# Gate rows of a mixture of experts spread by products of turned gates, and a new order of the first two images

## The reference

```
h = concat(cls_tok, fourier_features(x) @ W.T)            # (8, 1025, 64)
h = h + causal_attention(layernorm(h), WQ, WK, WV)
e = layernorm(h)
w = softmax(mean(e, axis=0) @ Wr + br)                    # gates: token x 8 experts, shared by all images
y = for each expert: relu(bn(relu(bn(e @ W1 + b1)) @ W2 + b2)) @ Wo + bo
h = h + sum over experts of w * y
```

## Time and profile before

| | us |
|---|---|
| three runs | 418.02, 421.12, 422.26 (median 421.12) |
| profiled execution, its own time | 418.62 |
| its span, first to last instruction | 416.8 |
| mean granted TensorE clock | 0.969 of full |
| PE busy | 371.0 (89%) |
| DVE, ACT, POOL busy | 274.4, 200.9, 116.8 |

### The profile page before, as it was taken

The page is one execution under the profiler, slowest core; times in us unless marked ns, Lnnn a source line. Parts: engine busy times, 40 slices in busy tenths (PEclk is TensorE's granted clock), DMA queues, the critical chain, the costliest instruction groups (busy, mean ns, idle before and its releaser), DMA issues. The chain is left out here.

```text
span 416.8 us, 8088 instructions
## 1 busy us (share of the span) xinstructions
PE 371.0 (89%) x2716; PEld 175.0 (42%) x2716; DVE 274.4 (66%) x582; ACT 200.9 (48%) x387; POOL 116.8 (28%) x197
## 2 busy tenths in 40 slices
PE   5887899999999999999999967857978999999985
PEld 3554244445345444434435434424456433333332
DVE  3132667777877977967967978797334365655665
ACT  0233255455555546546546555456714565556521
POOL 4050202415414414324325324226300730000000
PEclk9989699999999999999999999999958999999999
DMA  6989901801800900900000000000000010011112
GB/s 150 221 156 221 171 2 40 165 0 39 165 2 17 186 0 1 200 0 0 0 0 2 2 1 0 2 1 2 2 0 0 3 27 16 12 26 27 27 27 50
DMA packets 29085, 20.42 MB, mean 49 GB/s; under 512 B 12376, under 2 KB 28928, under 8 KB 29056
## 3 DMA queue, kind: packets, MB, share of 16 engines
q1 hardware_dynamic: 28448, 19.91, 23.7%
q10 hardware_dynamic: 608, 0.12, 0.2%
HBM read 17.93 MB, written 2.10 MB: 48 GB/s over the span
## 5 line engine op out<-in xcount | busy, mean ns | idle before, releaser
L777 DVE TENSOR_REDUCE rmax<-Sp 128x1 f32<-128x1024 f32 x64 | 78.2, 1222 | 27.4 <-PE Sp L1135 26.7
L1135 PE MATMUL Sp<-eT,G 64*64 64x512 f32 x512 | 70.6, 620 | 22.3 <-issue 18.1
L503 ACT ACTIVATE PT<-PTp 128x512 f32<-128x512 f32 (+2 forms) x96 | 43.5, 489 | 48.4 <-PE PTp L1150 48.2
L402 POOL TENSOR_SCALAR_AFFINE_SELECT EP<-EP 128x128 f32<-128x128 f32 x64 | 23.0, 360 | 149.1 <-ACT EP L556 149.1
L556 ACT ACTIVATE EP<-Sp,negm 128x128 f32<-128x128 f32 (+3 forms) x64 | 47.7, 745 | 24.0 <-DVE negm L779 23.5
L787 DVE SCALAR_TENSOR_TENSOR EP<-Sp,EP 128x128 f32<-128x128 f32 (+3 forms) x64 | 48.1, 751 | 15.4 <-PE PTp L1150 9.4
L1150 PEld LDWEIGHTS PTp<-ident,EP 128*128 128x128 f32 x288 | 31.8, 143 | 43.9 <-issue 36.9
L1150 PE MATMUL PTp<-ident,EP 128*128 128x128 f32 x288 | 45.3, 285 | 3.5 <-DVE EP L787 2.8
L1135 PEld LDWEIGHTS Sp<-eT,G 64*64 64x64 f32 x512 | 14.9, 132 | 49.6 <-issue 49.6
L1168 PE MATMUL MM<-PT,e 128*64 128x512 f32 (+1 forms) x192 | 34.2, 491 | 0.5 <-ACT PT L503 0.3
L979 DVE SCALAR_TENSOR_TENSOR PT<-PTp,negc,XW 128x512 f32<-128x512 f32 x30 | 21.1, 746 | 18.1 <-PE PTp L1305 12.3
(11 more groups left out here) (264 smaller groups left out, 585.8 us busy)
## 6 DMA issues: line engine op xcount, KB each, us to landing
XW<-in_x_dram SPq DMA_DIRECT2D x6, 1024.0 KB, 10.0
X<-in_x_dram SPq DMA_DIRECT2D x6, 1024.0 KB, 10.8
out_dram<-xc SPq DMA_DIRECT2D x16, 128.0 KB, 2.0
XW<-in_x_dram SPq DMA_DIRECT2D x2, 576.0 KB, 8.8
X<-in_x_dram SPq DMA_DIRECT2D x2, 576.0 KB, 14.2
XW<-in_x_dram SPq DMA_DIRECT2D x2, 448.0 KB, 11.7
X<-in_x_dram SPq DMA_DIRECT2D x2, 448.0 KB, 13.7
EP<-in_L_tok_W_dram SPq DMA_DIRECT2D x2, 144.0 KB, 3.2
```

Of the source, the lines that this page charges most:

```text
L402: pool.affine_select(out=blk_, in_=blk_, compare_op=ALU.is_ge, fill=0.0, base=0, pattern=[[-1, 128]], channel_multiplier=1).then_inc(tri_d ...
L503: return act.activation(dst, src, ACT.Copy)
L777: dve.reduce_max(rmax[:, t:t + 1], Sp[t % 2][:, :], AX).then_inc(max_done, 1)
L1135: ins = pe.matmul(Sp[t % 2][64 * s:64 * s + 64, CH * c:CH * c + CH], G[q][rows, 128 * t + 64 * s:128 * t + 64 * s + 64], eT[q][rows, :], **ON)
```

## The change

1. **Start.** The five products of the class token move from in front of image 2 to behind `g_pair(0, 0)`, into a bank of Sp, and the batch-norm rows go to Sp too. Both parts of image 2 now run with only the batch-norm rows between them, ahead of `e_turn`. `score(0, 0, 0)` now comes before `sr_turn`, which waits for `agT`. On ACT the copies of the class token's vectors move behind `g_copy`; on DVE the two steps for `w00` move behind the first image's attention.
2. **Gate rows.** POOL makes a constant `pick` at the start (two copies of 64x512). DVE writes the gates twice over into `gwp` (two products of 128x64 elements), PE turns them with four transposes (and one for the class token), ACT and DVE copy one half each to `wT`, and the gate rows of a pair are two products of 64 x 128 x 512, `pick` against `wT`, into Sp. ACT's copy to WB stays.
3. **Bias.** The bias product is made for two halves (16 products instead of 8) and moves from before the second layer norm to behind `layer2(0, 0)`, beside the softmax. The product with the gates is four of 128 columns and one of 64 instead of nine of 64, from the same `wT`; the nine transposes are gone.
4. **Order of the experts.** `layer1(1, 2)` moves in front of the last logits, `layer2(0, 1)` uses the banks M0 and M1, DVE's layer norm of the eighth image comes before the first logits' step, `c_l2` no longer waits for that step, and `layer1(1, 3)` moves behind `c_l3`. SP loads `bo` twice. POOL clears two more buffers.

```diff
-        wT = EPs[0:NEXP, 0:9 * 128]
-        gx = [EPs[:, 1152:2176]..., prod[...]]
+        wT = EPs[:, 0:CH]
+        wTc = EPs[0:NEXP, CH:CH + 128]
...
# POOL
+            pool.wait_ge(turn_high, 1)
+            for r in range(2):
+                rows = slice(64 * r, 64 * r + 64)
+                pool.tensor_copy(pick[rows, :, :, :], eye2[rows, 0:2 * NEXP].rearrange("p (c a s) -> p a c s", c=2, s=2)[:, :, :, r]
+                                 .unsqueeze(3).to_broadcast([64, NPAIR, 2, D])).then_inc(pool_steps, 1)
...
# DVE
             ln2_ss(b)
+            ln2_e(b)
             dve.wait_ge(pe_steps, nth("q_lf", 1))
...
-            ln2_e(b)
...
+            for r in range(2):
+                dve.tensor_tensor(gwp[:, :, r, 0:2 * NEXP]..., gl9[:, 0:NT, :]..., gs9[:, 2, 0:NT]..., ALU.mult)
+            dve.tensor_tensor(gw9[:, NT:NT + 1, :], ...)
+            dve.wait_ge(pe_steps, nth("q_wT", 1))
+            dve.tensor_copy(wT[:, 256:CH], M1[:, 0:256]).then_inc(dve_steps, 1)
+            dve.wait_ge(pe_steps, nth("q_bo", 1))
+            dve.tensor_tensor(bo2[0:2 * NEXP, :, :], ..., ALU.add).then_inc(dve_steps, 1)
-            def spread(i): ...
...
# PE, start
-            pe.wait_ge(act_steps, nth("c_e0Tc", 1))
-            pe.matmul(M1[:, 0:D], e0T[:, :], AT32[:, :], **ON)
...
+            for n in range(8):
+                y_part(1, n, 8)
+            pe.wait_ge(act_steps, nth("c_e0Tc", 1))
+            e_turn(0, 0)
+            g_pair(0, 0)
+            pe.wait_ge(act_steps, nth("bn_c2", 2))
+            for c in range(2):
+                pe.matmul(Q0[64 * c:64 * c + 64, 384:385], AT32[:, :], e0T[:, 0:1], **ON)
...
+            score(0, 0, 0)
+            pe.wait_ge(act_steps, nth("c_ag", 2))
             sr_turn(0, 0)
# PE, experts
             def weight_rows(i):
...
-                for t in range(NT):
-                    ins = pe.transpose((MM, Sp[0], Sp[1], MM)[i][:, 128 * t:128 * t + 128], gx[i % 2][:, t, :], ident[:, :])
+                for r in range(2):
+                    rows = slice(64 * r, 64 * r + 64)
+                    ins = pe.matmul(L1p[1 - i % 2][r], pick[rows, i, :, :], wT[rows, :], **ON)
...
             layer2(0, 0)
+            pe.wait_ge(h1_done, 14)
+            for c in range(2):
+                for e in range(NEXP):
+                    k = 24 * e + 8 - 8 * c
+                    ins = pe.matmul(L1p[0][0][0:2 * NEXP, D * c:D * c + D], c2sel[:, k:k + 16], Wof[0:64, e, :],
+                                    start=(e == 0), stop=(e == NEXP - 1))
+            ins.then_inc(pe_steps, 1)
+            pe.wait_ge(dve_steps, nth("q_w", 2))
+            for i in range(QG):
+                pe.transpose((M0, M1)[i // 2][:, 128 * (i % 2):128 * (i % 2) + 128], gwp[:, i, :, :], ident[:, :])
...
             weight_rows(0)
+            for i in range(QG):
+                pe.matmul(M0[:, 128 * i:128 * i + 128], wT[0:64, 128 * i:128 * i + 128], bo2[:, :, :], **ON)
+            pe.matmul(M1[:, 0:D], wTc[:, :], bo2[0:NEXP, 0, :], **ON).then_inc(pe_steps, 1)
             weight_rows(1)
+            layer2(0, 1)
             weight_rows(2)
+            layer2(0, 2)
             weight_rows(3)
```

More of the change, by code:

```diff
@@ L85, in tower @@
         e32 = [sb(f"e32_{i}", [128, NT, D]) for i in range(2)]
-        prod = sb("prod", [128, NT, 2, D])
+        gwp = sb("gwp", [128, QG, 2, 64])
+        pick = sb("pick", [128, NPAIR, 2, D])
+        bo2 = sb("bo2", [64, 2, D])
         xc2 = sb("xc2", [128, NT, D])
@@ L925, in _ @@
             body(0, 0, first=True)
+            dve.wait_ge(act_steps, nth("c_vecc", 2))
+            dve.wait_ge(dve_steps, nth("c_e0", 1))
+            dve.tensor_tensor(c1B[:, :], e0B[:, :], ag[:, 1, :], ALU.mult).then_inc(dve_steps, 1)
+            dve.wait_ge(dve_steps, nth("c_w00p", 1))
+            dve.reduce_sum(w00[:, :], c1B[:, :], AX).then_inc(dve_steps, 1)
             with dve.Fori(0, NB // 2 - 1) as j:
@@ L937, in _ @@
             ln2_centre(b)
-            dve.wait_ge(pe_steps, nth("k_eT", 1))
-            dve.tensor_tensor(bo_s[:, :], M0[0:NEXP, 288:288 + D], bo_s[:, :], ALU.add).then_inc(dve_steps, 1)
             ln2_ss(b)
+            ln2_e(b)
             dve.wait_ge(pe_steps, nth("q_lf", 1))
@@ L1283, in layer1 @@
                     pe.wait_ge(p_done, at(8 * NB - 1 + p))
-                if b == 1 and p == 2:
-                    pe.wait_ge(act_steps, nth("q_wTc", 2))
+                if (b, p) in ((1, 3), (2, 0)):
+                    pe.wait_ge(act_steps, nth("q_bcc", 6 - p if b == 1 else 4))
                 pe.wait_ge(h1_done, at(8 * b + 2 * p - 2))
@@ L1296, in layer2 @@
                 if b == 0 and p == 0:
-                    pe.wait_ge(pt_done, at(NCH * NB))
-                pe.wait_ge(t_done, at(8 * b + 2 * p - (2 if NPAIR * b + p >= NPAIR * (NB - 1) - 1 else 0)))
+                    pe.wait_ge(dve_steps, nth("c_m", 2))
+                elif b == 0 and p == 1:
+                    pe.wait_ge(dve_steps, nth("q_wbc", 1))
+                elif b == 0 and p == 2:
+                    pe.wait_ge(t_done, 2)
+                else:
+                    pe.wait_ge(t_done, at(8 * b + 2 * p - (2 if NPAIR * b + p >= NPAIR * (NB - 1) - 1 else 0)))
                 if (b, p) == (NB - 2, 3):
@@ L1374, in _ @@
                     rows = slice(64 * s, 64 * s + 64)
-                    ins = pe.matmul((M0, M1)[s][0:64, 384 + 8 * p:392 + 8 * p], W2f[rows, p, :], h1c[rows, p, :], **ON)
+                    ins = pe.matmul(PTp[s][0:64, 8 * p:8 * p + 8], W2f[rows, p, :], h1c[rows, p, :], **ON)
             ins.then_inc(pe_steps, 1)
-            pe.wait_ge(dve_steps, nth("c_m", 2))
+            pe.wait_ge(ot_done, at(2 * NB))
             e2_turn(b)
+            layer1(1, 2)
             pe.wait_ge(e2t_done, at(NB))
+            pe.wait_ge(dve_steps, nth("q_lga", 1))
             for i in range(QG):
@@ L1409, in _ @@
             ins.then_inc(pe_steps, 1)
-            layer1(2, 1)
+            layer1(1, 3)
+            layer2(0, 3)
+            layer1(2, 0)
             pe.wait_ge(act_steps, nth("c_y", 1))
             pe.transpose(M1[0:8, 192:192 + D], yTc[:, :], ident[0:64, 0:64]).then_inc(pe_steps, 1)
+            layer1(2, 1)
             layer3(0, 0)
```

180 lines of the change are left out of this document (73 added, 107 removed).

## The result

The changed kernel is slower: 425.29 us (median of 20 runs, 421.16 to 427.61) against 421.94 (20 runs, 418.02 to 425.92), ratio 1.0077 with a 95% interval of 1.0044 to 1.0109. That is a loss of 0.8%, clear of the noise but less than the one per cent that the prediction calls slower. The prediction was 415.4, faster; the range ended at 420.0.

The account below looks back on a forecast made before the run. PE bounds the tail, partly at 1.2 GHz; the first row maximum opens attention. Start 0.8 plus tail 3.8 make 4.6 off: 414.0 from the profiled 418.62, set at 415.4 from 420.0; range 411.0 to 420.0.

Parts of the forecast that it names:

- The start, 1.3 earlier at the first row maximum: Opening of attention: first row maximum at 37.5 against 38.78, with image 2 begun earlier and at full clock.
- The 0.8 that was to be left at the end: Start's net gain: 1.0 taken after the 43 to 49 slow stretch, less 0.2 for DVE's `w00` steps.
- Rival B: Start pays nothing, through slow clock in image 2's first part or a later slow stretch: 416.2 us, chance 0.20.
- unless a slow stretch takes it back: Attention: moving the first row maximum moves all of it, except where 1.2 GHz stretches such as 43 to 49 intervene.
- the rise of the clock between 312.7 and 315.6: Tail: PE unbroken from 309.5, so clock rises up to 2.9 us sooner than 315.6, third layer 4.5 to 3.0 earlier.
- the rule was weighed: Tail: whether removing 32 full transposes removes what raised the clock; late and absent rises were kept among the cases.
- C: Rival: tail's clock rises near 319 because bias products are narrow; tail gains 1.4, start 0.4: 418.2 us, chance 0.16.
- D: Rival: 1.2 GHz up to the third layer, 427 us, chance 0.08; decides from a rise after 322.4, 0.5 per us.
- The bias products, "1.7 at full, 3.4 at half clock": Tail, behind the first `layer2`: sixteen bias products on PE's path, 1.7 us at full clock or 3.4 at half.
- The sum from the first gate-row pair to the third layer, 11.05: Tail at full clock: 10.8 us of PE's own work plus 0.25 for a DVE add, ACT's copies and `gated` hidden.
- 3.8 for the tail: Third layer's first product 3.8 us earlier, between 4.5 and 3.0, as transposes and copy rounds go, less bias products.
- The base, 420.0: Time the gain was taken from: the average of four times, above the profiled 418.62 and below the median 421.12.

Follow-up runs that it names:

- the start alone: The kernel before with only the new order of the start, old tail kept: 421.76 against 422.34 us, ratio 1.0004.
- bo_early: The changed kernel with the sixteen bias products put back in front of the class token's turn: median 421.39 against 422.34 us for the kernel before.
- wait_fill: The changed kernel plus five groups of four unread 64x64x512 products in the tail: 416.54 against 422.34 us for the kernel before, ratio 0.9895.
- before_fill: The kernel before plus five groups of four unread 64x64x512 products in its tail: 423.49 against 421.51 us, ratio 1.0013.
- turn_fill: The changed kernel plus five groups of eight unread 128x128 transposes in the tail: 416.11 against 422.78 us for the kernel before, ratio 0.9869.
- fill_fit: The changed kernel, bias products early, unread products in tail, attention's start and idle steps of images 7 and 8: 410.58 against 422.49 us (before), ratio 0.9748.
- fill_more: The changed kernel, bias products early, unread products in tail, attention's start and nearly every step of images 7 and 8: 415.26 against 422.78 us (before).
- bo_wide: The changed kernel with an unread 64x64x64 companion product for the bias products, in another quadrant: 432.67 against 422.78 us for the kernel before, ratio 1.0237.
- narrow_fill: The changed kernel plus five groups in the tail, each one unread product 8 columns wide, 512 moving: 426.01 against 421.51 us for the kernel before.

## Why the prediction was wrong

- **The start, 1.3 earlier at the first row maximum:** right, 1.44 from the H copy on, with the predicted steps: image 2's two parts at full clock, PE without a wait for the load of X or for POOL's diagonal. For the load the prediction had a weak reason: the last two loads of X took 13.4 and 13.9 us in the kernel before, nearer the long end of 10.5 to 15.0 than the short one. The 0.8 that was to be left at the end is not seen: the start alone has ratio 1.0004, with an interval of 2 us either way that cannot tell 0.8 from nothing. Rival B (the time is given back to the clock) fits, but it was not shown.
- **The attention, which moves by what moves its beginning "unless a slow stretch takes it back":** the exception was the rule. Its slow stretches (6.8 or 20.5 us at 1.2 GHz) came and went among kernels with the same list of instructions there, and move it by 4 to 5 us. The prediction looked at one execution of the kernel before, among the best of its kind (0.969), and reckoned with no slow stretch in attention but the one at 43 to 49.
- **The tail, the rise of the clock between 312.7 and 315.6, because "PE is now unbroken from 309.5":** this is the step that failed. PE was unbroken from 305 to 322, and the clock rose at 332. The first second-layer product stands 6.0 us later in this execution than in the one of before (315.44 against 309.45), so on the prediction's scale the rise came at 326, and behind the last logits the clock was down for 18.5 us in place of 8.2. I took unbroken work as enough. What stood before the rise in the earlier trace rows were transposes and nothing else, and I had written that down where the rule was weighed and given a later rise 24 chances in 100, 16 for a rise near 319 (C) and 8 for none before the third layer (D). It is their mechanism, with D's place right and its decision point (a rise later than 322.4 costs) passed; the clock was back at 326 on that scale and not only at the third layer. By D's price of 0.5 per us of delay that is 1.8 later than before; with the 1.1 by which the sum below was too small it makes 2.9, and the third layer did come 2.9 later behind the last logits (25.72 against 22.82).
- **The bias products, "1.7 at full, 3.4 at half clock":** right in size, 3.59. What the prediction did not weigh is that they could have stayed off PE's path: put back in front of the layer norm they gave 3.9 us (`bo_early`), part of it by the clock.
- **The sum from the first gate-row pair to the third layer, 11.05:** at full clock it is 12.2 (`wait_fill`, 315.36 to 327.56), 1.1 more. PE shows no idle time in it. From the start of one group to the start of the next it is 1.01 to 1.06 where a gate-row pair is followed by a second layer and back, priced at 0.87, and the bias rows took 1.34, priced at 1.0: these terms were too small. Why a group takes longer there was not looked into.
- **A structural gain:** there is one. In `wait_fill` against `before_fill` it is some 1.5 to 2.5 us behind the last logits, by estimate. In the runs as they are, at equal time at 1.2 GHz the changed kernel would be some 1 us faster (mean 424.5 less 0.39 x 42.1 against 421.5 less 0.39 x 32.1); the 10 us more at 1.2 GHz cost 3.9. I forecast 3.8 for the tail with the clock back by 316 at the latest, and it was not.
- **The base, 420.0:** the kernel before has a median of 421.94 over 20 runs, so 1.9 of the 9.9 us between 415.4 and 425.29 are the base and not the change.

Not settled: why the attention's slow stretches come in some executions and not in others, whether the new start has a share in them, and what in the work of PE raises the clock.

## What to carry to other kernels

Before you take work away from TensorE, look at the clock in the same stretch and ask what brought it up: here 41 transposes were taken out and the clock stayed low behind them, and forty added as pure waste at earlier places (`turn_fill`) gave 9 us. That PE works without a pause on small products is no proof that its clock will rise. And where an engine's waits lie in a slow stretch, products that nobody reads can pay: with them in the attention's waits and a few groups in the tail, `fill_fit` came out 2.5% below the kernel before; with more of them outside the waits, as in `fill_more`, 4.7 us of that were lost again.

## What the runs showed of the hardware

- The clock of TensorE stayed at 1.2 GHz for 27 us in the changed kernel, with PE busy without a break in the first 17 of them (3.00 of 3.00 us in each of 309 to 312, 312 to 315 and 315 to 318), and in `bo_wide` for 34 us. In none of the six runs with five groups of eight 128x128 transposes was the mean clock below 0.973; with one product of 8 columns in place of each group, as long on PE, it was 0.945 to 0.963 in four of six.
- Runs of one and the same kernel differ with the clock: the kernel before from 418.04 (0.969) to 426.43 (0.945). One us at 1.2 GHz goes with 0.39 us of time over 45 runs, not 0.5; that some of it lies beside waits for other engines would fit, but was not shown.
- A 64x16 and a 64x64 product of 64 columns in opposite quadrants, one behind the other with new weights each, did not overlap: 0.72 us for a pair at 1.2 GHz, where the first kind alone takes 0.22 (sixteen in 3.59). Four quadrant products of 512 columns do: two such groups take 1.90 us in `wait_fill`, two single products 1.88 in `narrow_fill`.
